# Relation scores of the edges by products of digit one-hots in the mean stage, and 32 gathered tiles in the second neighbour sum, in a four-layer graph network

## The chip, the cores and the metric

The kernel is written in Bass and runs as one program on one core of a Trainium2 chip. The metric is the device time of one execution in microseconds (us). TensorE is called PE here (its weight loads PEld), VectorE DVE, ScalarE ACT, GpSimd POOL, and the engine that only issues DMAs SP.

## What is computed

The graph has 12500 nodes, 200000 edges sorted by destination, 128 features and 200 edge types. Four layers follow each other, each with a residual sum and a layer norm. The parts that matter here:

```python
summed = segment_sum(feature[src], dst)            # layer 0: mean over incoming edges
agg = summed / max(deg, 1); h = relu(agg @ W.T) + feature
out = w[0] * h                                     # layer 1: complex, 32 neighbours a node, twice
for k in range(deg): out = out + w[1 + k] * h[nbrs[:, k]]
a = hs @ Ws.T + h[dst] @ Wd.T + emb_rel[etype] @ Wr.T      # layer 2: attention
e = leaky_relu((a @ attn_fc2_w.T)[:, 0], 0.01)     # softmax over the edges of a node, weighted sum
```

The third term of `a`, once multiplied by `attn_fc2_w`, is one number for each of the 200 relations. The kernel has these 200 numbers early (`rel_score`, on every partition) and needs for each edge the number of its type (`edge_score`).

## The kernel before

Nodes lie in 98 tiles of 128. Edges lie in 1660 steps (`STEPS`) of 128, each of which belongs to one tile; edge data is held as 128 partitions by 1664 columns, one column a step. All five engines run hand-written programs in order, joined by semaphores. In time the stages are these:

- **Preparation** (to about 370 us of the span): indices, degrees, weights.
- **Mean stage** (about 367 to 2520 us): for every step POOL gathers 128 rows of x (`sum_gpsimd`, L1014, a ring of 14 slots), ACT makes a one-hot of the destinations in two passes (L1026, L1028, 8 slots), PE multiplies (L1039) into one of four banks of PSUM (`N_SUM_BANKS`), and DVE adds the bank to the tile's sum (L1072). PE's product of step i waits until the sum of step i-4 is taken, and DVE's program adds step i-2 where PE's has step i. The **sort** of the neighbour lists shares DVE, PE and ACT: a stage is an ACT copy of 2048 columns to PSUM (L1175) and two DVE operations of 2048 columns (L1098, L1099) or four of 1024 (L1107, L1108), a turn is four PE transposes (L1146) and an ACT copy (L1179). `weave` lays the 10 items of a small side computation (`evo_vector`) and 333 items of the sort evenly over the 1660 steps, so that an item comes every 4.84 steps whatever it costs. The sort begins with 80 stages in a row.
- **finish0** (to about 2730 us): the dense part of layer 0 and the first layer norm.
- **First neighbour sum** (about 2730 to 4994 us): two laps over 52 dense tiles (`DENSE`), each 98 products of 384 columns (L1413); the matrices of counts are built in the first lap (DVE one-hots L1386 and L1391, PE L1399, ACT L1405), stored, and read back in the second. The other 46 tiles are gathered by POOL (L1449) and reduced by DVE (L1471). The ends of tiles (L1551 and on, PE L1688 to L1695) are spread over both laps.
- **Second neighbour sum** (about 4994 to 6396 us, `window2_*`): `SECOND = 28` tiles are gathered: 4 batches a tile, 8 gathers a batch (L1743), three batch slots, each batch reduced by DVE (L1756). The 70 others are dense: 52 with stored counts, then 18 whose counts are built beside their products (32 groups a tile, from `b == ROUND` on).
- **Attention** (about 6400 to 8750 us) and the convolution of layer 3 (to the end).

The relation scores are made on DVE by `rel_vector`: 200 pairs of passes over 1660 columns, one that picks the edges of relation r (L1712) and one that adds them to `edge_score` (L1714). 70 pairs (`EARLY_RELATIONS`) are woven into the second lap of the first sum, 130 into the second sum up to the point where its counts are built; `hot_vector(ROUND)` waits for the last of them, and so do the load of the late entries on SP and the attention.

## Time and profile before

| | us |
|---|---|
| median of 3 runs | 10004.24 |
| lowest and highest | 9991.14, 10006.8 |
| span of the profiled execution | 9988.2 |
| busy: PE, DVE, ACT, POOL | 7824.2, 7971.0, 5963.0, 6961.9 |
| first neighbour sum, second lap (about) | 3907 to 4994 |
| second neighbour sum (about) | 4994 to 6396 |

The profiled execution's time is known by its span alone, 9988.2 us, which is 16 us under the median of the runs and 3 us under the lowest. In the profile, a group of instructions shows its busy time, the mean duration of one in ns, and the idle time of its engine just before them with what ended it. PEclk is the granted TensorE clock as a share of 2.4 GHz. Rows that end in "xN" count instructions. A matmul on f32 operands shows as two records.

### The profile page before, as it was taken

Reading aid. Unit: us, or ns where it says so; the run is one execution under the profiler, and the core shown is the slowest. Engines: PE = TensorE matmul, PEld = TensorE weight load, DVE = VectorE, ACT = ScalarE, POOL = GpSimd, SP = SyncE. Lnnn points to the kernel's source line nnn. Section 1 sums busy time; section 2 is a strip of 40 time slices with the busy share of each in tenths; the row PEclk is TensorE's granted clock in tenths of the full one; section 3 lists DMA queues with packets and bytes.
Section 4 is the critical chain, followed back from the end, with each engine's and each line's share of the span. In section 5 each row is a group of like instructions: output and inputs, shape, how many; then the busy total and the mean of one; then the engine's idle time right before and its main releaser. Section 6 shows DMA issues by size and latency. Waiting matters only on the chain.

```text
span 9988.2 us, 178573 instructions
## 1 busy us (share of the span) xinstructions
PE 7824.2 (78%) x39865; PEld 6121.3 (61%) x39865; DVE 7971.0 (80%) x24833; ACT 5963.0 (60%) x18344; POOL 6961.9 (70%) x7476
## 2 busy tenths in 40 slices
PE   4444555555799999898889989888888888848887
PEld 4333444444477777777677777666666666636665
DVE  7787556555878887999967768788888888899999
ACT  6777777777877774111100006688888888846665
POOL 0466777777078887777678877566666666649995
PEclk6555555555899999999999999855565565557876
DMA  2222222222588888887766662322222222210000
GB/s 52 54 48 48 53 53 53 53 53 53 189 253 239 243 238 267 287 289 280 247 250 224 224 214 61 81 49 49 49 50 49 49 50 49 50 28 1 1 1 27
DMA packets 530133, 1151.52 MB, mean 115 GB/s; under 512 B 147134, under 2 KB 398210, under 8 KB 508750
## 3 DMA queue, kind: packets, MB, share of 16 engines
q0 software_dynamic: 241872, 477.23, 19.9%
q10 hardware_dynamic: 22752, 517.02, 13.2%
q1 hardware_dynamic: 264478, 145.85, 5.5%
q8 instruction: 363, 5.95, 0.2%
q14 instruction: 668, 5.47, 0.2%
HBM read 886.72 MB, written 259.31 MB: 115 GB/s over the span
## 4 chain that ended last, share of the span: by engine, by line
DVE 24%; POOL 23%; PE 22%; issue 14%; ACT 11%; DVEq 3%; DMA 2%; SPq 1%; ACTq 0%; POOLq 0%
POOL onehot L2185 9%; PE bank L1413 7%; POOL step_data L1743 7%; POOL step_data L1449 4%; PE bank_tile L2042 3%; POOL gather_ring L1449 3%; ACT onehot L1028 2%; DVE keys L1099 2%; DVE keys L1108 2%; ACT onehot L1026 2%; PE bank L1039 2%; DVE keys L1471 2%; DVE arena L1072 2%; PE bank_tile L2052 2%; DVE keys L2022 2%
## 5 line engine op out<-in xcount | busy, mean ns | idle before, releaser
L1014 POOL DMA_INDIRECT gather_ring<-mean_rows,step_data x1660 | 1596.1, 961 | 784.3 <-PE bank L1039 288.2
L1039 PE MATMUL bank<-gather_ring,onehot 128*128 128x130 f32 x3320 | 1042.1, 460 | 1053.0 <-DVE arena L1072 724.8
L1413 PE MATMUL bank<-arena 128*128 128x384 bf16 x8526 | 1628.5, 330 | 30.4 <-DMA arena<-split_out 26.9
L1413 PE MATMUL bank<-arena,keys 128*128 128x384 bf16 x8526 | 1623.5, 330 | 11.8 <-DMA arena<-split_im 11.8
L1039 PEld LDWEIGHTS bank<-gather_ring,onehot 128*128 128x128 f32 x3320 | 805.8, 306 | 1279.1 <-issue 851.6
L1413 PEld LDWEIGHTS bank<-arena 128*128 128x128 bf16 x8526 | 1178.9, 139 | 289.8 <-issue 47.5
L1413 PEld LDWEIGHTS bank<-arena,keys 128*128 128x128 bf16 x8526 | 1177.4, 138 | 270.5 <-issue 24.7
L1743 POOL DMA_INDIRECT step_data<-next_rows,window_idx x896 | 1045.9, 1167 | 351.1 <-issue 263.9
L1449 POOL DMA_INDIRECT step_data<-hidden,window_idx x888 | 1060.9, 1195 | 293.9 <-issue 265.9
L1966 POOL DMA_INDIRECT gather_ring<-attention_rows,step_data x834 | 786.8, 943 | 435.5 <-PE bank_tile L2042 228.6
L1966 POOL DMA_INDIRECT keys<-attention_rows,step_data x826 | 779.3, 943 | 388.0 <-PE bank_tile L2042 227.1
L1072 DVE TENSOR_TENSOR arena<-arena,bank 128x130 f32 x1660 | 482.4, 291 | 690.4 <-PE bank L1039 528.1
L2185 POOL TENSOR_SCALAR onehot<-iota_row,step_data 128x128 f32<-128x128 f32 x1660 | 960.0, 604 | 0.3 <-PE bank_tile L2223 0.2
L2213 ACT ACTIVATE gather_ring<-gather_ring,window_idx 128x128 f32<-128x128 f32 x1660 | 666.1, 401 | 295.7 <-DVE gather_ring L2196 268.9
L1449 POOL DMA_INDIRECT gather_ring<-hidden,window_idx x584 | 694.6, 1189 | 177.9 <-issue 174.3
L2196 DVE SCALAR_TENSOR_TENSOR gather_ring<-first_row,keys,l3b 128x128 f32<-128x128 f32 x1660 | 710.4, 428 | 0.2
L1028 ACT ACTIVATE onehot<-onehot,ones 128x128 f32<-128x128 f32 x1660 | 666.6, 402 | 53.8
L1026 ACT ACTIVATE onehot<-iota_row,step_data 128x128 f32<-128x128 f32 x1660 | 642.7, 387 | 93.6 <-PE bank L1039 67.5
L2084 ACT ACTIVATE step_small<-arena,step_small 128x1 f32 x1660 | 491.3, 296 | 315.3 <-DVE step_small L2012 289.4
L2052 PE MATMUL bank_tile<-ident,keys 128*128 128x128 f32 x1328 | 582.6, 439 | 120.6 <-DVE keys L2022 112.7
L1204 ACT ACTIVATE small<-small,eps 128x1 f32<-128x1 f32 x392 | 119.9, 306 | 893.8 <-DVE small L1200 882.1
L2004 DVE SCALAR_TENSOR_TENSOR arena<-arena,step_small,bank_tile 128x129 f32 x1328 | 465.5, 351 | 207.3 <-ACT step_small L2084 96.9
(350 smaller groups left out, 20302.8 us busy)
## 6 DMA issues: line engine op xcount, KB each, us to landing
keys<-count_rows ACTq DMA_DIRECT2D x50, 3136.0 KB
arena<-count_rows ACTq DMA_DIRECT2D x50, 3136.0 KB
count_rows<-arena ACTq DMA_DIRECT2D x26, 3136.0 KB
count_rows<-keys ACTq DMA_DIRECT2D x26, 3136.0 KB
gather_ring<-mean_rows,step_data POOLq DMA_INDIRECT x1660, 2.5
step_data<-next_rows,window_idx POOLq DMA_INDIRECT x896
step_data<-hidden,window_idx POOLq DMA_INDIRECT x888
gather_ring<-attention_rows,step_data POOLq DMA_INDIRECT x834
```

Of the source, the lines that this page charges most:

```text
L1014: e.indirect_dma_start(ring_at(rings.slot(name, i), SUM_COLS, SUMS - 1), None, rows, bass.IndirectOffsetOnAxis(src_idx[:, i:i + 1], 0), bo ...
L1026: e.activation(h, iota_row[:, :], ACT.Abs, bias=dst_local[:, j:j + 1], scale=-1.0).then_inc(hot_made)
L1028: e.activation(h, h, ACT.Relu, bias=ones[:, 0:1], scale=-1.0).then_inc(hot_made)
L1039: e.matmul(pass_bank[i % N_SUM_BANKS][:, 0:SUMS], onehot[:, i % STEP_SLOTS, :], ring_at(rings.slot(name, i), SUM_COLS, SUMS), start=True, ...
L1072: e.tensor_tensor(part, part, pass_bank[j % N_SUM_BANKS][:, 0:SUMS], ALU.add).then_inc(step_added)
L1413: m = e.matmul(pass_bank[n % 2][:, 0:SPLIT_COLS], counts[t % 2][:, :, h], split[:, h, :], start=(h == 0), stop=(h == NODE_TILES - 1))
L1449: e.indirect_dma_start(first_rows(i)[:, a, :], None, hidden1, bass.IndirectOffsetOnAxis(gather_idx[:, k * GATHERED + j:k * GATHERED + j + ...
L1743: e.indirect_dma_start(batch_rows[:, i % BATCH_SLOTS, r, :], None, next_rows, bass.IndirectOffsetOnAxis(gather_idx[:, at:at + 1], 0), boun ...
L1966: e.indirect_dma_start(attention_row(j), None, attention_rows, bass.IndirectOffsetOnAxis(src_idx[:, j:j + 1], 0), bounds_check=None).then_inc(
L2052: e.transpose(turned_part(j), logit[:, s, :], ident[:, :]).then_inc(a_logit_turned)
L2185: e.tensor_scalar(onehot[:, j % CONV_SLOTS, :], iota_row[:, :], dst_local[:, j:j + 1], None, ALU.is_equal).then_inc(hot_made)
L2196: e.scalar_tensor_tensor(lines[:, j % CONV_SLOTS, :], first_row[:, :], edge_coef[:, j:j + 1], l3b1[:, :], ALU.mult, ALU.add).then_inc(conv ...
```

## The change

`rel_vector` is replaced. A relation is split into a high digit (type modulo 8) and a low digit (type divided by 8, 0 to 24). The edge types are also written to DRAM in row form and read back four rows at a time. For each of the 128 rows, DVE makes a one-hot of the high digits (104 partitions by 128 columns, bf16) and one of the low digits (128 by 25 by 13, bf16); PE multiplies the first with a table split into three bf16 pieces (three products of 325 columns, summed in the fourth bank); DVE multiplies the result with the second and sums 25 values for each of 13 columns. This runs beside the mean, in `weave`, between `evo_vector` and the sort. The scores go to DRAM and are loaded again at the start of the second sum, as the late entries are. The mean has three banks instead of four. `weave` now gives every side item a cost, and the 1660 steps are shared in proportion: a stage 66 (6.9 steps), a turn 8 (0.83), a rescale 24, a row of relations 14 (1.46), an item of `evo_vector` 15 (1.56). `SECOND` is 32: 66 dense tiles, 14 of them with counts built, and 128 more gathers.

```diff
+N_SUM_BANKS = 3
...
-SECOND = 28
+SECOND = 32
...
-EARLY_RELATIONS = 70
+REL_HIGHS = 8
+REL_LOWS = RELATIONS // REL_HIGHS
+REL_PARTS = REL_HIGHS * STEP_GROUPS
+REL_COLS = REL_LOWS * STEP_GROUPS
+REL_ROWS = 4
+REL_LOADS = P // REL_ROWS
+REL_ROOM = 164
+REL_ROW_SLOTS = 2
+STAGE_COST, SHORT_COST, TURN_COST, RESCALE_COST, REL_COST = 66, 15, 8, 24, 14
...
+def weave(main, side, main_total, costs):
+    total, spent, at = sum(costs), 0, 0
+    for done, _ in enumerate(main, 1):
+        while at < len(costs) and spent * main_total < done * total:
+            next(side)
+            spent, at = spent + costs[at], at + 1
+    for _ in side:
+        pass
...
-SORT_STAGES = len(SORT) + 1 + DEG // 4 + GROUPS // 4
+SIDE_COSTS = [SHORT_COST] * 10 + [REL_COST] * (P + 2) + [
+    {"stage": STAGE_COST, "turn": TURN_COST, "rescale": RESCALE_COST}[row[0]] for row in SORT] + [
+    STAGE_COST] + [TURN_COST] * (DEG // 4 + GROUPS // 4)
...
-            own().tensor_copy(edge_rows_f[s][:, 2 * P:], edge_rows_sb[s][:, 2 * P:]).then_inc(n.sem, n.up())
+            own().tensor_copy(type_staged[:, g * P:(g + 1) * P], edge_rows_sb[s][:, 2 * P:]).then_inc(n.sem, n.up())
...
+    def rel_vector(e):
...
+        own().tensor_copy(type_int, type_staged).then_inc(n.sem, n.up())
+        own().tensor_scalar(type_int, type_int, REL_HIGHS - 1, None, ALU.bitwise_and).then_inc(n.sem, n.up())
+        own().tensor_copy(type_staged, type_int).then_inc(n.sem, n.up())
+        mark["types_staged"] = n.n
+        own().tensor_copy(type_int, edge_type[:, :]).then_inc(n.sem, n.up())
+        own().tensor_scalar(type_int, type_int, REL_HIGHS.bit_length() - 1, None,
+                            ALU.logical_shift_right).then_inc(n.sem, n.up())
+        own().tensor_copy(edge_type[:, :], type_int).then_inc(n.sem, n.up())
+        yield
+        own().tensor_copy(rel_iota, iota_row[:, 0:REL_LOWS].rearrange("p (w o) -> p w o", o=1).to_broadcast(
...
+        e.wait_ge(rel_landed, 32 * REL_HIGHS)
+        rest = rel_block[0:REL_PARTS, :]
...
+        for k in range(PIECES):
+            own().tensor_copy(rel_pieces[k][0:REL_PARTS, :], rest).then_inc(n.sem, n.up())
+            if k < PIECES - 1:
+                own().tensor_tensor(rest, rest, rel_pieces[k][0:REL_PARTS, :], ALU.subtract).then_inc(n.sem, n.up())
+        mark["rel_pieces"] = n.n
...
+        for r in range(P + 1):
+            if r < P:
+                c, at = divmod(r, REL_ROWS)
+                if at == 0:
+                    e.wait_ge(type_landed[c % REL_ROW_SLOTS], 16 * (c // REL_ROW_SLOTS + 1))
+                if r >= 2:
+                    e.wait_ge(rel_summed, r - 1)
+                    e.wait_ge(rel_scored, 2 * r - 3)
+                e.tensor_scalar(rel_hot[r % 2][0:REL_PARTS, :],
+                                rel_rows[c % REL_ROW_SLOTS][0:REL_PARTS, at * P:(at + 1) * P],
+                                rel_high[0:REL_PARTS, 0:1], None, ALU.is_equal).then_inc(rel_hots)
+                e.tensor_tensor(
+                    rel_low[r % 2],
+                    low_digits[:, r:r + 1, :].to_broadcast([P, REL_LOWS, STEP_GROUPS]),
+                    rel_iota, ALU.is_equal).then_inc(rel_hots)
+            if r:
+                i = r - 1
+                e.wait_ge(rel_summed, r)
+                e.wait_ge(rel_hots, 2 * r)
+                if i:
+                    e.wait_ge(rel_scored, 2 * i)
+                e.tensor_tensor(rel_product, rel_sums, rel_low[i % 2].rearrange("p w g -> p (w g)"),
+                                ALU.mult).then_inc(rel_scored)
+                e.wait_ge(rel_scored, 2 * i + 1)
+                e.tensor_reduce(scores[:, i, :], rel_product.rearrange("p (w g) -> p g w", w=REL_LOWS), AX.X,
+                                ALU.add).then_inc(rel_scored)
+            yield
+    def rel_tensor(e):
+        yield
+        yield
+        e.wait_ge(rel_digits.sem, mark["rel_pieces"])
+        for r in range(P):
+            e.wait_ge(rel_hots, 2 * r + 1)
+            if r:
+                e.wait_ge(rel_scored, 2 * r - 1)
+            for k in range(PIECES):
+                m = e.matmul(rel_sums, rel_hot[r % 2][0:REL_PARTS, :], rel_pieces[k][0:REL_PARTS, :],
+                             start=(k == 0), stop=(k == PIECES - 1))
+            m.then_inc(rel_summed)
+            yield
+    def rel_sync(e):
+        e.wait_ge(prep_copies, ACT_WEIGHTS)
+        with nc.allow_non_contiguous_dma(reason="one element a row, once"):
+            for h in range(REL_HIGHS):
+                e.dma_start(rel_table[h * STEP_GROUPS:(h + 1) * STEP_GROUPS, :],
+                            rel_score[0:STEP_GROUPS, :].rearrange("p (w h) -> p w h", h=REL_HIGHS)[:, :, h]).then_inc(
+                    rel_landed, 16)
+        e.wait_ge(rel_digits.sem, mark["types_staged"])
+        for h in range(REL_HIGHS):
+            e.dma_start(type_rows[h * STEP_GROUPS:(h + 1) * STEP_GROUPS, :, :].rearrange("g p e -> p g e"),
+                        type_staged.rearrange("p (g e) -> p g e", g=STEP_GROUPS)).then_inc(rel_landed, 16)
+        e.wait_ge(rel_landed, 32 * REL_HIGHS)
+        for c in range(REL_LOADS):
+            s = c % REL_ROW_SLOTS
+            if c >= REL_ROW_SLOTS:
+                e.wait_ge(rel_hots, 2 * (c - REL_ROW_SLOTS + 1) * REL_ROWS)
+            e.dma_start(rel_rows[s][0:REL_PARTS, :].rearrange("p (r e) -> p r e", r=REL_ROWS),
+                        type_rows[:, c * REL_ROWS:(c + 1) * REL_ROWS, :]).then_inc(type_landed[s], 16)
+        e.wait_ge(rel_scored, 2 * P)
+        e.dma_start(score_rows[:, :], made_score).then_inc(entries_saved, 16)
...
-        own().memset(edge_score, 0.0).then_inc(n.sem, n.up())
-        for r in range(RELATIONS):
-            own().tensor_scalar(picked, edge_type[:, 0:STEPS], float(r), rel_score[:, r:r + 1], ALU.is_equal,
-                                ALU.mult).then_inc(n.sem, n.up())
-            own().tensor_tensor(edge_score, edge_score, picked, ALU.add).then_inc(n.sem, n.up())
-            yield
...
                 if b == ROUND:
-                    e.wait_ge(rel_steps.sem, mark["rel_end"])
-                    e.wait_ge(entries_back, 16)
+                    e.wait_ge(entries_back, 32)
...
+        e.wait_ge(digit_steps, DIGITS * DENSE)
+        e.dma_start(entries_late, entry_rows[:, :]).then_inc(entries_back, 16)
+        e.wait_ge(built, ROUND)
+        e.dma_start(edge_score, score_rows[:, 0:STEPS]).then_inc(entries_back, 16)
...
-                if t == DENSE - 4:
-                    e.wait_ge(rel_steps.sem, mark["rel_end"])
-                    e.dma_start(entries_late, entry_rows[:, :]).then_inc(entries_back, 16)
...
-        weave(sum_vector(e, "mean", 0, regs), itertools.chain(evo_vector(e), sort_vector(e)), STEPS, EVO_STAGES + SORT_STAGES)
+        weave(sum_vector(e, "mean", 0, regs), itertools.chain(evo_vector(e), rel_vector(e), sort_vector(e)), STEPS, SIDE_COSTS)
...
-        relations = rel_vector(e)
-        weave(first_vector(e), itertools.islice(relations, EARLY_RELATIONS), 2 * ROUND + HOT_AHEAD, EARLY_RELATIONS,
-              ROUND + HOT_AHEAD + GROUPS)
-        weave(window2_vector(e), relations, ROUND - 2 * HOT_AHEAD, RELATIONS - EARLY_RELATIONS)
+        for _ in first_vector(e):
+            pass
...
+        weave(sum_tensor(e, "mean", 0), itertools.chain(range(EVO_STAGES), rel_tensor(e), sort_tensor(e)), STEPS, SIDE_COSTS)
...
+        weave(sum_scalar(e, 0), itertools.chain(evo_scalar(e), range(P + 2), sort_scalar(e)), STEPS, SIDE_COSTS)
```

## Rows read from the trace of the kernel before

**Rows 1.** The page: busy tenths of DVE and POOL in 40 slices of 250 us.
```profile
DVE  7787556555878887999967768788888888899999
POOL 0466777777078887777678877566666666649995
```
**Rows 2.** Windows (busy PE, PEld, DVE, ACT, POOL; PEclk; DMA share; GB/s), mean stage.
```profile
450.00:950.00 500.00, 204.24 (x711) 175.21 (x709) 427.40 (x627) 388.67 (x790) 342.79 (x362) 0.50 0.22 48
1000.00:2500.00 1500.00, 830.24 (x2842) 654.77 (x2842) 872.25 (x1484) 1108.26 (x2590) 1139.65 (x1183) 0.53 0.24 53
```
**Rows 3.** Groups of instructions, 340 to 2300 us, forms kept apart.
```profile
L1014 POOL DMA_INDIRECT gather_ring<-mean_rows,step_data x1489 | 1431.0, 961 | 732.1 <-PE bank L1039 259.0 <-issue 243.5 <-DMA mean_rows<-edge_values 229.7
...
L1072 DVE TENSOR_TENSOR arena<-arena,bank 128x130 f32 x1487 | 432.2, 291 | 626.3 <-PE bank L1039 479.9 <-DVE arena L1072 145.1 <-issue 0.9
```
**Rows 4.** Line L1014: ns min/median/max, first and last start.
```profile
L1014 POOL DMA_INDIRECT gather_ring<-mean_rows,step_data x1660: 938/944/4672, 366.7 to 2516.4; - x185
```
**Rows 5.** The timeline after a stage of the sort: start us, us, what.
```profile
904.19 0.28 DVE L1072 TENSOR_TENSOR arena<-arena,bank 128x130 f32 x1
...
904.62 2.74 PE L1039 MATMUL bank<-gather_ring,onehot 128*128 128x130 f32 x10 [3.83 <-DVE arena L1072]
904.68 0.29 DVE L1072 TENSOR_TENSOR arena<-arena,bank 128x130 f32 x1 [0.20 <-DVE arena L1072]
...
906.36 2.28 DVE L1098 TENSOR_TENSOR keys<-keys,bank_tile 128x2048 f32<-128x2048 f32 x1
```
**Rows 6.** The two passes of a relation, by line.
```profile
L1712 DVE TENSOR_SCALAR window_idx<-edge_type,rel_score x200: 1052/1078/1309, 3934.5 to 5939.8; 128x1660 f32<-128x1660 bf16 x100
L1714 DVE TENSOR_TENSOR keys<-keys,window_idx x200: 1886/1887/1891, 3935.8 to 5940.9; 128x1660 f32<-128x1660 f32 x100
```
**Rows 7.** POOL's gathers in 3960 to 4950, 5100 to 5900 and 6000 to 6300 us.
```profile
L1449 POOL DMA_INDIRECT step_data<-hidden,window_idx x420 | 458.5, 1092 | 129.6 <-issue 125.8 <-DVE keys L1471 3.8
...
L1743 POOL DMA_INDIRECT step_data<-next_rows,window_idx x507 | 648.3, 1279 | 154.5 <-issue 154.2 <-DVE gather_ring L1756 0.3
...
L1743 POOL DMA_INDIRECT step_data<-next_rows,window_idx x218 | 211.8, 971 | 89.7 <-issue 59.4 <-DVE gather_ring L1756 30.4
```
**Rows 8.** The second lap: its window, and PE's longest wait there (us, times, longest).
```profile
3907.00:4994.00 1087.00, 956.51 (x5552) 775.65 (x5552) 997.71 (x1717) 125.40 (x380) 813.22 (x742) 0.95 0.78 278
...
PE bank_tile L1688 <- DVE turned_few L1567: 105.6, 45, 6.5
```
**Rows 9.** The second sum: lines L1743 and L1413; then windows of L1413 and of L1399.
```profile
L1743 POOL DMA_INDIRECT step_data<-next_rows,window_idx x896: 938/945/3022, 4998.6 to 6354.5; - x180
...
L1413 PE MATMUL bank<-arena,keys x8526: 325/326/528, 2774.2 to 6391.9; 128*128 128x384 bf16 x199
...
6000.00:6100.00 100.00, 93.61 (x435) 60.33 (x435) 1.00 0.25 64
...
6000.00:6100.00 100.00, 46.83 (x142) 16.00 (x143) 1.00 0.25 64
```
**Rows 10.** DVE groups of the whole span that are nearest to the new operations.
```profile
L2031 DVE TENSOR_SCALAR keys<-iota_half,step_data 128x128 bf16<-128x128 bf16 x1660 | 452.4, 273 | 6.3 <-issue 5.7 <-PE bank L2059 0.5
L1386 DVE TENSOR_TENSOR onehot<-arena,iota_quad 128x512 bf16<-128x512 bf16 x560 | 236.5, 422 | 254.5 <-PE bank_tile L1399 249.8 <-issue 0.2
...
L1756 DVE TENSOR_REDUCE gather_ring<-step_data 128x128 f32<-128x1024 f32 x112 | 219.1, 1956 | 115.9 <-DMA step_data<-next_rows,window_idx 115.9
...
L601 DVE TENSOR_TENSOR keys<-arena,iota_half 125x784 bf16<-125x784 bf16 x120 | 116.2, 968 | 0.0
```
**Rows 11.** SP's issue of 12544 single elements; a window inside the load of x.
```profile
L986 SPq DMA_DIRECT2D mean_rows<-edge_values x1: 387/387/387, 348.7 to 348.7; - x1
...
385.00:390.00 5.00, 3.07 (x9) 1.98 (x9) 1.88 (x10) 4.81 (x13) 3.78 (x5) 0.50 1.05 290
```
**Rows 12.** The timeline at 5045 us: a relation's pass and a gather.
```profile
5045.57 1.89 DVE L1714 TENSOR_TENSOR keys<-keys,window_idx 128x1660 f32<-128x1660 f32 x1
5045.97 2.31 POOL L1743 DMA_INDIRECT step_data<-next_rows,window_idx  x1 [0.30 <-issue]
```

More of the change, by code:

```diff
@@ L120, in landed @@
         return self.sems[s], 16 * (self.base[name][s] + sum(self.sizes[name][s:i + 1:self.slots[name]]))
-def weave(main, side, main_total, side_total, after=0):
-    done_main = done_side = 0
-    for _ in main:
-        done_main += 1
-        while side is not None and done_side * (main_total - after) < (done_main - after) * side_total:
-            if next(side, StopIteration) is StopIteration:
-                side = None
-            done_side += 1
-    if side is not None:
-        for _ in side:
-            pass
+def weave(main, side, main_total, costs):
[6 more added lines that the diff above has]
+        pass
 def ending(now, hop):
@@ L472, in program @@
     batch_added = sem("gathered_batch_added")
-    rel_steps = Tally(sem("relation_score_steps"))
+    rel_digits = Tally(sem("relation_digit_steps"))
+    rel_landed = sem("relation_tables_landed")
+    type_landed = [sem(f"type_rows_landed{i}") for i in range(REL_ROW_SLOTS)]
+    rel_hots = sem("relation_onehots")
+    rel_summed = sem("relation_products")
+    rel_scored = sem("relation_score_steps")
     hist_high = sem("source_high_onehots")
@@ L835, in prep_tensor_program @@
             e.wait_ge(prep_vector.sem, mark["edges_read", g])
-            for k in range(3):
+            for k in range(2):
                 e.transpose(tile_bank[2 + s][:, k * P:(k + 1) * P], edge_rows_f[s][:, k * P:(k + 1) * P],
                             ident[:, :]).then_inc(made)
+            e.transpose(tile_bank[2 + s][:, 2 * P:2 * P + P // 2].bitcast(BF16), type_staged[:, g * P:(g + 1) * P],
+                        ident_half[:, :]).then_inc(made)
             if g >= 1:
@@ L2316, in tensor @@
         e.wait_ge(prep_vector.sem, mark["setup"])
-        weave(sum_tensor(e, "mean", 0), itertools.chain(range(EVO_STAGES), sort_tensor(e)), STEPS, EVO_STAGES + SORT_STAGES)
+        weave(sum_tensor(e, "mean", 0), itertools.chain(range(EVO_STAGES), rel_tensor(e), sort_tensor(e)), STEPS, SIDE_COSTS)
         finish0_tensor(e)
@@ L2342, in sync @@
         x_program(e)
+        rel_sync(e)
         sort_sync(e)
```

65 lines of the change are left out of this document (51 added, 14 removed).

## The prediction

> **What bounds the kernel now.** I read the page's slices first [rows 1]: DVE stands at 9 in slices 17 to 20, where 70 of the relation pairs lie, and at 6 or 7 in 21 to 24 with the other 130; POOL stands at 7 or 8 through most of the mean stage and of both sums. Then the windows.
>
> In the mean stage POOL sets the pace. A gather takes 0.944 us with about 0.30 between two: 1.25 us a step at best. From 366.7 to 2516.4 us its 1660 gathers take 2150 us, 1.296 each, so 75 us lie above that floor [rows 4]. The window from 450 to 950, where the sort's 80 first stages lie, has 362 gathers in 500 us, 1.38 each, with DVE busy for 427; the one from 1000 to 2500 has 1183, 1.268 each, with DVE at 58% [rows 2]. So DVE bounds the stretch where stages come densely, POOL the rest. A stage blocks DVE for 4.6 us, and 0.29 us adds follow it, 0.20 apart [rows 5]; POOL's ring of 14 hides about 17 us of delay.
>
> In the second lap of the first sum, DVE is busy for 998 of 1087 us and POOL makes 742 gathers, 1.42 us each with hardly a wait, since each takes 1.092 instead of 0.944 [rows 7, 8]. PE waits 105.6 us for ends that come late from DVE [rows 8]. In the second sum the gathers take 1.279 us while relations run and 0.971 after [rows 7]; DVE waits for their landing (115.9 us in all) [rows 10]. There POOL, slowed by DVE, holds the others. After 6000 us PE is full: 435 products and 142 counts in 100 us, 0.173 us each [rows 9].
>
> **Part 1, the 200 pairs go.** DVE loses 200 x (1.078 + 1.887) = 593 us [rows 6], of which 70 pairs, 207 us, lie in the lap and 130, 386 us, in the second sum. DVE time by itself is worth nothing; two things follow from it.
>
> In the lap, POOL's gathers fall from 1.09 to about 0.96 us, 1.26 with the gap: 742 x (1.42 - 1.26) = 119 us less for POOL. PE gets back up to the 105.6 us it waits, and has then no more idle time: it needs about 1087 - 106 = 981 us. Next late is PE itself, at full work. I take 95 us off the lap; bounds 40 (the waits of PE are only moved, as DVE still has some 790 us of work there) and 110.
>
> **Part 2, 32 gathered tiles.** POOL now has 1024 gathers in the second sum. They start at 4998.6 and end at 6354.5, and the stage ends some 40 us later [rows 9]. Without relations one costs 0.96 + 0.30: 1024 x 1.262 = 1292 us, and 11 us that POOL waits at the start for its slots come again. POOL ends at 4998.6 + 1303 = 6302, the stage at about 6340: 56 us earlier. PE has 66 x 98 = 6468 products and 14 x 32 = 448 counts, 6916 x 0.173 = 1196 us, ended well before that; so the four tiles more lie on POOL's path, and it becomes the one bound of the stage. Bounds: 20 (gathers at 1.30) and 75 us (1.25).
>
> **Part 3, the relation rows enter the mean stage.** The new code lies at steps 16 to 206 of 1660: costs 150 + 130 x 14 of a total of 15936, that is 9.6 a step.
>
> Before the first row stand six passes over 1664 columns on DVE, priced by [rows 6] at 1.1 to 1.9 us, some 9 us; then a wait for 16 DMAs. Eight are small. The other eight write the digits to DRAM in 13312 pieces of 256 bytes, and SP issues them after the load of x (6.4 MB at 290 GB/s, to about 400) [rows 11]. The nearest price below is 12544 single elements in 366.7 - 348.7 = 18 us [rows 4, 11]; above, x itself, 12500 pieces of 512 bytes in 22 us, and half as much again is 33. The ten early items now come every 1.56 steps, so DVE reaches the digits at about 407, has them at 412 and the first rows of digits back at about 440. POOL's ring covers 17 us of that stop. The 32 reads of four rows are prefetched by 4 to 8 rows, over 10 us: nothing. If that cover goes, a landing of 2 to 3 us stands on each fourth row, about 80 us in all.
>
> One row on DVE: one-hot of 128 columns 0.27; one-hot of 325 columns 0.37 (bounds 422 x 325/512 = 0.27 and 968 x 325/784 = 0.40); product of 325 columns 0.49 (slope between 0.291 at 130 and 1.887 at 1660 columns); sum 0.62 (325/1024 of 1.956; bounds 0.49 at the product's price and 0.75) [rows 3, 6, 10]. That is 1.75, and 0.20 between the dependent two [rows 5]: 1.95. With 1.46 adds of 0.29 it is 2.4 to 2.5 us, against 1.82 that POOL needs for 1.46 steps. So DVE becomes the bound there. PE can add to it. Its three products of 325 columns at half clock [rows 2] take 3 x 0.173 x 2 x 325/386 = 0.88 us, and with three banks its mean product of step i waits for the add of step i-3, which DVE makes only one step ahead. In a row that spans two steps (46% of them) the chain is: sum 0.82, add 0.29, mean product 0.7, three products 0.9, product 0.49, latencies: 3.3 us. A row with one step takes 2.24. The mean is 2.73. I take 2.6, between this and DVE's own 2.47; bounds 1.9 and 3.2.
>
> 128 x 2.6 = 333: the rows end at 773. What is left is 1455 steps, of which 14 are already gathered: 1441 x 1.265 = 1823 (as 1.268 now; dense stages have 6.9 steps, 8.6 us, for 4.6 of stage and some 3.4 of adds, so three banks just suffice). Turns get only 0.83 steps, 1.04 us, less than their transposes and a mean product take on PE; the ring absorbs eight in a row. The stage ends at 2600 against 2520: **80 us later**. Bounds: 243 for the rows and 1.25 after, 32 us earlier; 410 and 1.30, 207 us later.
>
> A rule bears on these rows. One gather that began beside an addition of two SBUF operands took 2.31 us instead of 0.94 [rows 12]. The Trainium skill (GPSIMD Engine Reference, Key points) says that GpSimd shares its SBUF interfaces with VectorE and contends with instructions in a two-port mode or with two SBUF inputs; by that, row and rule agree, and it speaks against the change: the one-hot of 325 columns has two SBUF inputs. By rows 12 the two one-hots would hold POOL for up to 0.64 us a row, 1.82 + 0.64 = 2.46: hidden behind DVE's 2.6, but it takes most of the gain away should rows be cheap.
>
> Everything else I put at nothing: preparation swaps a cast for a cast; two loads of 0.2 and 0.8 MB at the start of the second sum lie beside 30 us of waiting for the split rows; ACT has no new work in the rows, and SP waits in them with nothing urgent behind it (the sort's entries come at its end).
>
> **Sum.** +80 - 95 - 56 = -71. The profiled execution's 9988 becomes 9917. The median of the runs lies 16 us above its span, so I forecast 10004 - 71 = **9933 us**. A measurement of this kernel can tell about 0.2%, 20 us, from no change.
>
> **Rivals.**
> - *Rows at POOL's pace* (0.17). If sum and one-hot stand at their low bounds and PE keeps ahead, the mean stage ends 32 us early: -32 - 95 - 56 = -183, 9821. For it: PE at half clock is busy for only 41% of 450 to 950 [rows 2]. Against: 1.95 + 0.42 is over 1.82 by any middle price.
> - *Rows held by the exchange of DVE and PE* (0.19), the other side. Each row passes DVE, PE, DVE, and the three banks tie the mean to the same chain. At 3.7 us a row the stage ends 80 + 128 x 1.1 = 220 us later: +69, 10073. It decides from 3.3 us a row: 80 + 90 is then over 151 + 19. For it: PE already waits behind DVE's adds for 3.83 us at a time [rows 5]. Against: one-step rows don't have the long chain.
> - *The sums give back little* (0.16). The lap yields only 40, as PE is just as busy, and the second sum 30, as 128 gathers fill the room: +80 - 70 = +10, 10014. For it: PE is busy for 957 of the lap's 1087 us [rows 8]. Against: its 105.6 us of waiting end in DVE's work.
> - That relations still stand in the sums can't be: their loop is gone.
>
> **How the numbers follow.** My forecast has 0.48. Faster by over 0.2%: 0.48 + 0.17 and 0.01 of the third, 0.66. Within: 0.13 of the third. Slower: 0.19 and 0.02 of the third, 0.21. The forecast's own range, from its bounds, is 9870 to 9980; with the rivals up to two in ten left out it reaches from 9830 to 10050.
>
> **What would show it.** Right: the last mean gather near 2597, rows of relations from about 440 to 773 with some 2.6 us between two products of DVE, POOL under 1.30 us a gather up to there lost and 1.265 after; gathers of 0.95 to 0.97 us in both sums; the lap at about 990 us; POOL without waits in the second sum and PE with some. Wrong: rows under 2 or over 3.3 us, DVE stopped for over 60 us before the first row, the mean stage above 1.30 after the rows (turns or three banks), or a second sum that ends no sooner than now.

## The result and the profile after

The changed kernel takes **10085.93 us**, median of 4 runs (10082.44 to 10087.5), against 10000.3 us of the kernel before in the same session (9991.14 to 10006.8): a ratio of **1.0085**, 95% interval 1.0071 to 1.01. It is slower. The forecast was 9933, the range ended at 10050, and slower had 0.21. The profiled execution has a span of 10080.7 us, 92.5 more than the 9988.2 of before. In six of the twelve sessions on record the kernel before itself took 10.9 to 11.0 ms instead of 10.0, so each run below is set against the kernel before of its own session, and only runs within a session, or from sessions in which it took 10.0 ms, are compared.

First the slices of the page, which answer to [rows 1]: DVE is no longer at 9 in slices 17 to 20 and only at 5 to 3 in 21 to 24, but in the mean stage POOL has come down too, from 7 to 6 in slices 5 to 10.

```profile
DVE  7776666666687888688853336788888888899999
...
POOL 0256666666617888777767777666666666649995
```

Then the gathers of the mean stage (min/median/max ns, first and last start), which answer to [rows 4].

```profile
L1051 POOL DMA_INDIRECT gather_ring<-mean_rows,step_data x1660: 938/944/4668, 374.3 to 2801.6; - x185
```

The last one starts at 2801.6 us instead of 2516.4: 285 us later, where 80 were forecast. Windows of the changed kernel (busy PE, PEld, DVE, ACT, POOL; PEclk; DMA share; GB/s): the rows of relations, the sort behind them, the second lap of the first sum, the second sum.

```profile
450.00:750.00 300.00, 224.44 (x714) 131.54 (x714) 234.53 (x657) 143.71 (x355) 167.62 (x178) 0.50 0.23 53
800.00:2500.00 1700.00, 701.72 (x2782) 626.82 (x2782) 1085.26 (x1691) 1186.00 (x2648) 1152.69 (x1199) 0.55 0.22 47
4194.00:5170.00 976.00, 923.55 (x5552) 771.81 (x5552) 798.49 (x1574) 125.82 (x380) 714.85 (x744) 0.99 0.86 310
5170.00:6500.00 1330.00, 1200.18 (x7210) 978.06 (x7210) 640.21 (x1953) 258.22 (x645) 976.51 (x1028) 0.96 0.58 197
```

From 800 to 2500 us there are 1199 gathers, **1.42 us each**; before it was 1.268 [rows 2]. No engine is full: ACT is at 70%, POOL 68%, DVE 64%, PE 41%. The lap lasts 976 us instead of 1087 [rows 8], with PE busy for 95% of it. The second sum goes from 5177.1 to the last product at 6488.3, 1311 us, where it was 4998.6 to 6391.9, 1393 [rows 9]. The balance: +285 in the mean stage, -111 in the lap, -82 in the second sum, together +92; the first lap and all that follows the sums stayed.

The waits of the changed kernel from 800 to 2750 us (us in all, times, longest) say who stands still in that mean stage.

```profile
PE bank L1076 <- DVE arena L1109: 1132.9, 200, 13.1
ACT onehot L1063 <- PE bank L1076: 512.5, 184, 6.0
POOL gather_ring L1051 <- PE bank L1076: 356.1, 484, 6.0
...
DVE keys L1239 <- ACT bank_tile L1317: 182.4, 100, 7.6
DVE keys L1248 <- ACT bank_tile L1317: 175.2, 81, 6.8
```

It is a ring: PE waits for DVE, ACT and POOL wait for PE, and DVE waits for ACT. The two rows at the end are the new ones. They are the sort's own operations waiting for ACT's copy of the stage, 357.6 us together; the same two waits of the kernel before (L1098 and L1107 on L1175) come to 32.9 us in that window. The timeline of one cycle of the changed kernel (start us, us, engine, line; in brackets the idle time before it) shows how the ring closes.

```profile
1449.98 0.28 DVE L1109 TENSOR_TENSOR arena<-arena,bank 128x130 f32 x1
1450.41 3.72 PE L1076 MATMUL bank<-gather_ring,onehot 128*128 128x130 f32 x14 [5.60 <-DVE arena L1109]
...
1451.22 0.40 ACT L1063 ACTIVATE onehot<-iota_row,step_data 128x128 f32<-128x128 f32 x1 [2.74 <-PE bank L1076]
...
1451.96 0.39 ACT L1063 ACTIVATE onehot<-iota_row,step_data 128x128 f32<-128x128 f32 x1
...
1452.69 0.39 ACT L1063 ACTIVATE onehot<-iota_row,step_data 128x128 f32<-128x128 f32 x1
1452.92 0.29 DVE L1109 TENSOR_TENSOR arena<-arena,bank 128x130 f32 x1 [0.20 <-DVE arena L1109]
...
1453.41 1.86 ACT L1317 ACTIVATE bank_tile<-keys 128x2048 f32<-128x2048 f32 x1
...
1455.31 2.29 DVE L1239 TENSOR_TENSOR keys<-keys,bank_tile 128x2048 f32<-128x2048 f32 x1 [2.10 <-ACT bank_tile L1317]
...
1457.51 2.28 DVE L1240 TENSOR_TENSOR keys<-keys,bank_tile 128x2048 f32<-128x2048 f32 x1
...
1459.71 0.28 DVE L1109 TENSOR_TENSOR arena<-arena,bank 128x130 f32 x1
```

At 1449.98 DVE leaves its block (the two operations of a stage, in which it takes no sums) and takes seven sums, 0.49 us apart, to 1453.21. PE had stood for 5.60 us, since all three banks were full; ACT had stood for 2.74, since its eight one-hots were made and none used. The stage's input has been ready since the block ended, but its copy starts only at 1453.41: in ACT's program three one-hots stand ahead of it, and each needs a product of PE. Then DVE waits 2.10 us for the copy. A cycle is 3.23 (sums) + 2.10 + 4.40 (block) = 9.73 us for seven steps, 1.39 a step.

### The profile page after: what moved, and what is told of

Same layout as the page of the kernel before. It is cut to its first block, busy times and chain, and to the rows that moved or that the text cites. A ratio compares the mean times of both kernels' runs of the same rounds, so it can differ in the third digit from the quotient of the medians.

```text
span 10080.7 us, 178575 instructions
## 1 busy us (share of the span) xinstructions
PE 7676.8 (76%) x39729; PEld 6052.8 (60%) x39729; DVE 7613.9 (76%) x24805; ACT 5912.3 (59%) x18216; POOL 6791.2 (67%) x7604
## 4 chain that ended last, share of the span: by engine, by line
POOL 29%; PE 19%; DVE 18%; issue 14%; ACT 13%; DMA 3%; DVEq 2%; SPq 1%; ACTq 0%; POOLq 0%
POOL onehot L2307 10%; POOL step_data L1865 8%; POOL step_data L1591 7%; POOL gather_ring L1591 4%; PE bank L1555 4%; ACT bank_tile L1317 3%; PE bank_tile L2164 3%; PE bank L1076 3%; ACT onehot L1065 2%; DVE keys L1240 2%; ACT onehot L1063 2%; DVE keys L1249 2%; PE bank_tile L2174 2%; DMA step_data<-hidden,window_idx 2%; DVE keys L2144 2%
## 5 line engine op out<-in xcount | busy, mean ns | idle before, releaser
L1076 PE MATMUL bank<-gather_ring,onehot 128*128 128x130 f32 x3320 | 948.6, 451 | 1320.5 <-DVE arena L1109 1214.7
L1555 PE MATMUL bank<-arena 128*128 128x384 bf16 x8330 | 1579.2, 329 | 28.6 <-DMA arena<-split_out 26.5
L1555 PE MATMUL bank<-arena,keys 128*128 128x384 bf16 x8330 | 1567.7, 328 | 10.0 <-DMA arena<-split_im 10.0
L1555 PEld LDWEIGHTS bank<-arena 128*128 128x128 bf16 x8330 | 1149.6, 138 | 275.7 <-issue 43.5
L1555 PEld LDWEIGHTS bank<-arena,keys 128*128 128x128 bf16 x8330 | 1147.6, 138 | 250.1 <-issue 20.7
L1865 POOL DMA_INDIRECT step_data<-next_rows,window_idx x1024 | 972.7, 950 | 351.4 <-issue 309.3
L1591 POOL DMA_INDIRECT step_data<-hidden,window_idx x888 | 999.3, 1125 | 293.6 <-issue 265.2
L1591 POOL DMA_INDIRECT gather_ring<-hidden,window_idx x584 | 655.9, 1123 | 177.9 <-issue 176.4
```

The lines of the kernel that those rows point to most:

```text
L1076: e.matmul(pass_bank[i % N_SUM_BANKS][:, 0:SUMS], onehot[:, i % STEP_SLOTS, :], ring_at(rings.slot(name, i), SUM_COLS, SUMS), start=True, ...
L1555: m = e.matmul(pass_bank[n % 2][:, 0:SPLIT_COLS], counts[t % 2][:, :, h], split[:, h, :], start=(h == 0), stop=(h == NODE_TILES - 1))
L1591: e.indirect_dma_start(first_rows(i)[:, a, :], None, hidden1, bass.IndirectOffsetOnAxis(gather_idx[:, k * GATHERED + j:k * GATHERED + j + ...
L1865: e.indirect_dma_start(batch_rows[:, i % BATCH_SLOTS, r, :], None, next_rows, bass.IndirectOffsetOnAxis(gather_idx[:, at:at + 1], 0), boun ...
```

## The experiments

**Theory A.** What counts is how far ACT can get while DVE is in its block. PE stops after as many products as there are banks, ACT after eight one-hots more (the eight slots), and since it makes one-hots `HOT_LEAD` = 5 steps ahead, the copy that stands s steps behind the block in the program is reached only if s is at most banks + 6 - lead (8 slots less the 2 steps by which DVE's sums lag): 5 in the kernel before, 4 after. Stages come every 4.84 steps before and every 6.9 after. So both edits, the third bank given away and the weave by costs, push the copy behind DVE's sums. **Theory B:** the weave alone does it. **Theory C** (used later): the missing bank itself does it, whatever ACT's order.

### Three banks alone, in the kernel before

```diff
-    N_SUM_BANKS = len(pass_bank)
+    N_SUM_BANKS = 3
```

> The kernel before with three banks for the mean instead of four, and nothing else. Theory A (the sort's copy on ScalarE stands in program order behind one-hots that wait for TensorE's products, and these for banks that VectorE has yet to add; so banks and the number of steps between two stages decide together): in runs of stages a five-step cycle gets one one-hot later, 0.7 us, the mean stage ends 60 to 130 us later than 2520, the time rises by as much. Theory B (the turns' small share of steps and the weights of the weave alone slow the changed kernel, banks are irrelevant): the mean stage ends within 20 us of 2520.

11220.37 us against 11033.23, +187. Again, on another chip:

> The kernel before with three banks for the mean, taken again. Theory A: in runs of stages the copy waits for one one-hot more in a cycle with five steps, and the block and its adds were the bound there already: the mean stage ends 60 to 130 us after 2520. Theory B (three banks suffice at any spacing): within 20 us.

11084.8 against 10905.17, +180. Both are more than the 60 to 130 us that theory A had given. A third time:

> The kernel before with three banks of the mean instead of four (N_SUM_BANKS), nothing else. Theory A (the copy of a sort stage stands on ScalarE behind one-hots that wait for a bank): the copy can stand at most 4 steps ahead instead of 5, and stages come every 4.84 steps, so a part of it falls behind each dense stage: the last mean gather from 2516 to 2560-2700 and the time from 10004 to 10050-10180. The theory of the prediction (three banks just suffice): 2516-2530, 10004-10020.

**10174.12 us** (3 runs) against 9996.34: 1.0177, 1.0157 to 1.0197. The gathers of this kernel:

```profile
L1014 POOL DMA_INDIRECT gather_ring<-mean_rows,step_data x1660: 938/944/4584, 368.0 to 2692.4; - x185
```

its waits from 400 to 2500 us:

```profile
ACT onehot L1026 <- PE bank L1039: 439.3, 171, 5.9
...
DVE keys L1107 <- ACT bank_tile L1175: 119.0, 84, 3.3
DVE keys L1098 <- ACT bank_tile L1175: 114.4, 87, 2.8
```

and the same waits of the kernel before with its four banks:

```profile
ACT onehot L1026 <- PE bank L1039: 63.0, 86, 3.4
DVE keys L1107 <- ACT bank_tile L1175: 20.2, 17, 3.3
DVE keys L1098 <- ACT bank_tile L1175: 14.8, 19, 2.9
```

One bank less costs 178 us, and the last gather comes 176 us later. DVE's wait for the copy grows by 198 us, ACT's for PE by 376. Nothing else was touched: even at the old spacing of the stages three banks don't suffice.

### The weave by costs alone, in the kernel before

```diff
-        weave(sum_vector(e, "mean", 0, regs), itertools.chain(evo_vector(e), sort_vector(e)), STEPS, EVO_STAGES + SORT_STAGES)
+        weave_costs(sum_vector(e, "mean", 0, regs), itertools.chain(evo_vector(e), sort_vector(e)), STEPS, SIDE_COSTS)
```

(the same for PE and ACT; costs as in the change, without the rows)

> The kernel before, its mean woven by the costs of the change (stage 66, turn 8, rescale 24, early item 15), four banks, relation passes where they were. A stage then has 7.8 steps, a turn 0.94. Theory A: the copy waits for some three one-hots after VectorE's block, but a cycle has 9.7 us of gathers to hide it in: the mean stage ends between 2470 and 2550 us. Theory B: turns that get 0.94 steps slow the stretches with turns to over 1.40 us a step, the mean stage ends after 2650.

11082.46 us against 11033.23, +49. Again:

> The kernel before woven by the costs of the change, four banks, taken again. Theory A: 7.8 steps lie between stages, the copy comes three one-hots late, about as long as 9.7 us of gathers can hide: the mean stage ends between 2470 and 2550. Theory B (the turns with 0.94 steps each are too tight): it ends after 2650.

10926.3 against 10905.17, +21. Theory B, that the weave alone makes the loss, is not supported by these single runs. The last gathers came at 2832.2 and 2812.0, past the 2470 to 2550 of theory A and where the rival of too tight turns had put them (after 2650); but no trace shows where the kernel before has its last gather when it takes 10.9 ms or more, so this decides nothing. DVE does wait for the copy in both (128.4 and 130.1 us from 800 to 2750, where the kernel before at 9988.2 waits 32.9), so the weave isn't free of A's effect with four banks either; a run against 10.0 ms would be needed for its size.

### The changed kernel with an even sort, and with a lead of 2

```diff
-STAGE_COST, SHORT_COST, TURN_COST, RESCALE_COST, REL_COST = 66, 15, 8, 24, 14
+STAGE_COST, SHORT_COST, TURN_COST, RESCALE_COST, REL_COST = 42, 15, 42, 42, 14
```

> The changed kernel with the same cost, 42, for each item of the sort (4.4 steps each), three banks. Theory A: the copy is hardly late, but VectorE's block and 4.4 adds take 6.7 to 7 us against 5.5 us of gathers, 1.55 us a step in 190 stages, and 1.25 in the rest: the mean stage ends at 2780 to 2830, no gain. Theory B (turns too tight is what slows it): it ends 100 us or more earlier than 2805.

11583.89 us against 11033.23, last gather at 3034.9: inconclusive, as the changed kernel itself was not run against 11033.23.

```diff
-    HOT_LEAD, ADD_LAG = 5, 2
+    HOT_LEAD, ADD_LAG = 2, 2
```

This kernel, the changed one with a lead of 2, was run in five sessions.

> The changed kernel with the one-hots made two steps ahead in program order instead of five. Theory A: ScalarE comes to the copy three steps earlier, so the copy starts as soon as VectorE's block ends and the 2 us that VectorE waits for it are gone; a stage's cycle falls from 9.73 us to what 6.9 gathers take, 8.6 us; the mean stage ends at 2570 to 2620 instead of 2805, the time is about 9860 to 9910. Theory B: no change, within 20 us.

> The changed kernel with the one-hots two steps ahead instead of five, three banks, taken again while the kernel before runs at its usual 10000 us. Theory A (the copy stands behind one-hots that wait for banks): the copy starts when VectorE's block ends, a stage's cycle falls from 9.73 to about 8.6 us, the mean stage ends at 2570 to 2620. Rival C (the shorter lead starves TensorE of one-hots where turns and relation rows lie): it ends above 2700.

> The changed kernel, three banks, with the one-hots two steps ahead instead of five. Theory A (the copy stands behind one-hots that wait for banks): the copy starts when VectorE's block ends, a stage's cycle falls from 9.73 to about 8.6 us, the mean stage ends at 2570 to 2620. Rival C (the shorter lead starves TensorE of one-hots): it ends above 2700.

> The changed kernel (three banks) with the destination one-hots made 2 instead of 5 steps ahead (HOT_LEAD), nothing else. Theory A (the copy of a sort stage stands on ScalarE behind one-hots that wait for a bank): with three banks and a lead of 2 the copy can stand 7 steps ahead, as with four banks and a lead of 3, so it starts right behind the block; DVE's wait for the copy, 357.6 us in all from 800 to 2750 us in the changed kernel, falls under 120; the last mean gather moves from 2802 to 2640-2720 and the time from 10086 to 9925-10005. Theory C (the bank itself is what is missing: PE stands still in the block after three products, not ScalarE's order): no gain, 2780-2820 and 10060-10100. Theory D (a lead of 2 starves PE of one-hots): over 2820.

> Again the changed kernel (three banks) with a one-hot lead of 2 instead of 5. Theory A (the copy stands behind one-hots that wait for a bank, so a shorter lead cures three banks as well as four): last mean gather 2640-2720 instead of 2802, time 9925-10005. Theory C (the missing bank itself holds PE in the block, whatever ScalarE's order): 2780-2820, 10060-10100. Theory D (a lead of 2 starves PE of one-hots): over 2820.

One run each in the first three: 11487.65 against 11033.23, 11346.06 against 10905.17, 11345.68 against 10898.65. The last two, of three runs each: 11464.7 against 11022.18 (1.0408, 1.0388 to 1.0429) and 11338.63 against 10898.14 (1.0412, 1.0391 to 1.0433). It is slower than the kernel before in all five; as the changed kernel wasn't run in them, the totals decide nothing between A and C, and whether a lead of 2 leaves PE short of one-hots (theory D) stays open. A stretch of the fourth run's timeline shows the mechanism of A all the same:

```profile
1456.54 0.28 DVE L1109 TENSOR_TENSOR arena<-arena,bank 128x130 f32 x1
1456.65 1.88 ACT L1317 ACTIVATE bank_tile<-keys 128x2048 f32<-128x2048 f32 x1 [1.33 <-DVE keys L1240]
...
1460.10 2.28 DVE L1239 TENSOR_TENSOR keys<-keys,bank_tile 128x2048 f32<-128x2048 f32 x1
...
1464.49 0.28 DVE L1109 TENSOR_TENSOR arena<-arena,bank 128x130 f32 x1
```

Now ACT waits for DVE, not DVE for ACT: the copy starts 0.11 us after the block, and a cycle of seven steps lasts 7.95 us instead of 9.73, with three banks.

### A fourth bank in the changed kernel

The fourth bank holds the rows' products only until the rows end; from step 240 on the mean can have it.

```diff
+    FOUR_FROM = 240
+    def sum_bank(i):
+        return pass_bank[i % (N_SUM_BANKS if i < FOUR_FROM else 4)]
...
-                if i >= N_SUM_BANKS:
-                    e.wait_ge(step_added, lap_ * STEPS + i - N_SUM_BANKS + 1)
+                if i == FOUR_FROM + 3:
+                    e.wait_ge(rel_scored, 2 * P)
+                banks = N_SUM_BANKS if i < FOUR_FROM + 3 else 4
+                if i >= banks:
+                    e.wait_ge(step_added, lap_ * STEPS + i - banks + 1)
```

> The changed kernel with a fourth bank for the mean from step 240 on, when the relation rows have left it. Theory A (ScalarE's copy stands behind one-hots that wait for banks): one more product can be made in VectorE's block, so the copy starts one one-hot earlier, 0.7 us of 9.7 a stage, over 190 stages some 140 us: the mean stage ends near 2650 to 2690 instead of 2805, the time is 9930 to 9980. Theory B (the turns' small share of steps slows it): within 20 us of the changed kernel.

**9965.72 us** (4 runs) against 10008.17: 0.9957, 0.9938 to 0.9977. The last gather comes at 2669.3, 132 us earlier than in the changed kernel. DVE's waits for the copy are 234.5 us from 800 to 2600 us (239.8 to 2750, against 357.6):

```profile
DVE keys L1255 <- ACT bank_tile L1324: 120.9, 81, 6.6
DVE keys L1246 <- ACT bank_tile L1324: 113.6, 98, 7.2
```

This restores the limit of 5 steps but not the spacing of 6.9, and half the wait for the copy is left in a cycle at the same place: 1.08 us of 9.12, where it was 2.10 of 9.73. That fits A, but C as well.

### Four banks and a lead of 3

```diff
-    HOT_LEAD, ADD_LAG = 5, 2
+    HOT_LEAD, ADD_LAG = 3, 2
```

This stands on top of the fourth bank of the run before. It ran three times. The first two:

> The changed kernel with the fourth bank from step 240 on and the one-hots three steps ahead. Theory A: by one bank and two steps of lead the copy is no more behind a waiting one-hot; a stage costs what its 6.9 gathers take; the mean stage ends at 2560 to 2600, the time is 9860 to 9900. Rival C (the shorter lead starves TensorE): no better than with the fourth bank alone, 9966.

> The changed kernel with the fourth bank from step 240 on and the one-hots three steps ahead, taken again. Theory A: the copy of a stage is no more behind a waiting one-hot; a stage costs what its 6.9 gathers take, 8.6 us; the mean stage ends at 2560 to 2600, the time is 9860 to 9900. Rival C (the shorter lead starves TensorE of one-hots): no better than with the fourth bank alone, 9966.

11334.23 against 10905.17 and 11316.83 against 10898.65, 4.0% and 3.9% slower than the kernel before; without the changed kernel beside them they decide nothing between the theories. The third:

> The changed kernel with a fourth bank from step 240 on (as in the run before) and destination one-hots made 3 instead of 5 steps ahead of the gather. Theory A (the copy of a sort stage stands on ScalarE behind one-hots that wait for a bank): with a lead of 3 and four banks the copy can stand up to 7 steps ahead, so it starts as soon as the last DVE operation of the block before it ends; the 1.08 us that DVE waits for the copy in each stage falls to under 0.3, a cycle of 7 steps from 9.12 to about 8.8 us (DVE's gap gone, then POOL's 7 x 1.25), the last mean gather moves from 2669 to 2610-2650 and the time to 9900-9950. Theory B (the weave by costs holds the stages, whatever the lead): 2669 and 9966 stay. Theory C (the shorter lead starves PE of one-hots): later than 2700, over 9990.

**9860.95 us** (3 runs) against 9997.11: 0.9864, 0.9845 to 0.9883, faster than theory A said. The last gather comes at 2581.4. From 800 to 2750 us DVE's waits for the copy are 52.2 us, and POOL makes 1344 gathers in the 1700 us from 800 to 2500, 1.265 each: it is the bound again.

### Three banks and a lead of 3: A against C

The changed kernel with the one line above, and nothing else.

> The changed kernel (three banks) with a one-hot lead of 3 instead of 5, nothing else. A fourth bank gave 132 us of the mean stage with a lead of 5, and the shorter lead then another 88. Theory A (what counts is how far the stage's copy can stand ahead on ScalarE, banks plus slots less lead): three banks and a lead of 3 let it stand 6 ahead, one more than four banks and a lead of 5, so the last mean gather comes at 2600-2669 instead of 2802 and the time is 9880-9966. Theory C (the missing bank itself holds PE in the block, whatever ScalarE's order): at most a third of the 220 us, 2730-2810 and 10020-10095.

**9863.49 us** (3 runs, 9859.24 to 9865.84) against 9995.54: 0.987, 0.9851 to 0.9889. Its gathers:

```profile
L1051 POOL DMA_INDIRECT gather_ring<-mean_rows,step_data x1660: 938/944/4603, 370.5 to 2581.8; - x185
```

and its waits from 800 to 2750 us:

```profile
PE bank L1076 <- DVE arena L1109: 710.4, 199, 10.8
ACT onehot L1063 <- PE bank L1076: 256.3, 197, 4.5
...
DVE keys L1248 <- ACT bank_tile L1317: 54.6, 52, 6.8
```

With L1239's 44.1 us DVE waits for the copy for 98.7 us instead of 357.6. The timeline shows one one-hot ahead of the copy where there were three:

```profile
1460.73 0.40 ACT L1063 ACTIVATE onehot<-iota_row,step_data 128x128 f32<-128x128 f32 x1 [1.28 <-PE bank L1076]
...
1461.48 1.86 ACT L1317 ACTIVATE bank_tile<-keys 128x2048 f32<-128x2048 f32 x1
...
1463.37 2.29 DVE L1239 TENSOR_TENSOR keys<-keys,bank_tile 128x2048 f32<-128x2048 f32 x1 [0.23 <-ACT bank_tile L1317]
```

C falls: without a fourth bank the mean stage is 220 us shorter, as short as with one (2581.8 and 2581.4), and even a little shorter than A had said (2600 to 2669). What the missing bank does, it does through ACT's order. At either spacing of the stages, the larger the limit, the earlier the last gather, until POOL is the bound:

| kernel | banks, lead | limit | stages every | last gather | time |
|---|---|---|---|---|---|
| before | 4, 5 | 5 | 4.84 | 2516.4 | 10000 |
| before, three banks | 3, 5 | 4 | 4.84 | 2692.4 | 10174 |
| changed | 3, 5 | 4 | 6.9 | 2801.6 | 10086 |
| changed, fourth bank | 4, 5 | 5 | 6.9 | 2669.3 | 9966 |
| changed, lead of 3 | 3, 3 | 6 | 6.9 | 2581.8 | 9863 |
| changed, both | 4, 3 | 7 | 6.9 | 2581.4 | 9861 |

### A lead of 3 in the kernel before

```diff
-    HOT_LEAD, ADD_LAG = 5, 2
+    HOT_LEAD, ADD_LAG = 3, 2
```

> The kernel before (four banks, relations in the sums, weave by count) with the destination one-hots made 3 instead of 5 steps ahead, nothing else. If the shorter lead helps only because the weave by costs packs up to 7 steps between two stages, it gives nothing here, where stages come every 4.84 steps and the copy can already stand 5 ahead: 2505-2525 for the last mean gather, 9990-10010. If the one-hots that wait for PE's banks hold ScalarE here too, the mean stage nears POOL's own pace of 1.25 us: 2445-2490, 9930-9980. If a lead of 3 starves PE where DVE's blocks come densely: over 2540 and 10020.

9991.7 us (9 runs) against 9993.21 (11 runs): 0.9997, 0.9986 to 1.0007. Last gather at 2516.7. DVE's waits for the copy from 800 to 2750 us are 26.8 us here, against 32.9 in the kernel before: with a limit of 5 and stages every 4.84 steps there is hardly a wait to remove, so the gain of the shorter lead belongs to the changed kernel. It follows that the spacing of 6.9 has a price with four banks too: the 88 us from 2669.3 to 2581.4. Freed of the waits, the change is worth -132 us (9863.49 - 9995.54).

### 28 gathered tiles instead of 32

```diff
-SECOND = 32
+SECOND = 28
```

(with a lead of 3)

> The changed kernel with a one-hot lead of 3 and 28 gathered tiles in the second sum instead of 32: the change without its second size. If POOL bounds the second sum with 32 tiles (1024 gathers of 0.95 and 0.30 us from 4959 to 6253, PE busy for 1197 of 1310 us), then with 28 its 896 gathers end after 1130 us, and PE with 520 more products and counts, some 87 us, needs 1284 of work and becomes the bound: the last dense product comes 1285 to 1330 us after the start instead of 1313, and the time is 9835-9880, no more than 20 us from 9863.5. If the four tiles more were worth what the prediction's second part says of them (the whole of its 56 us), it is 9900-9920.

11210.01 us against 10896.02, which can't be set beside the 9863.49: POOL waits for DVE here for 555.2 us in the second sum, which with 32 tiles, at 9863.49, it did for 11.0. How the 82 us of the second sum divide between the relations that left and the four tiles stays open.

## Why the prediction was wrong

**What failed: the pace after the rows.** Part 3 took "1441 x 1.265 (as 1.268 now; dense stages have 6.9 steps, 8.6 us, for 4.6 of stage and some 3.4 of adds, so three banks just suffice)". Block and sums were right (4.40 and 3.23 us), but they don't follow each other: 2.10 us of waiting for ACT's copy lie between them. 9.73 us for seven steps is 1.39 a step. Over all that follows the rows, the gathers took 2058 us (743.2 to 2801.6), 1.42 each, where 1823 had been foretold: this term was 235 us too small. The rows had come 30 us early, so the last gather missed the 2597 foretold by 205. The term's upper bound of 1.30 was the mean of the old stage, not a bound of the new one. I had named three banks as what could make the stage slow and never asked through whom: the sum counted the bank's effect on PE and DVE, and not on the third engine, whose program has the copy behind one-hots that need PE. The kernel before gave a sign of it: ACT's one-hots waited for PE for 63 us with a longest wait of 3.4. The lead of 3 shows that this was the step: it alone brings the pace to 1344 gathers in 1700 us, 1.265, and the last gather to 2581.8, against the 2597 foretold.

**Part 3, the rows: right.** DVE's wait for the digits' way through DRAM is 12.8 us (28 had been left for it, from 412 to 440), and the first product of DVE starts at 431.6. The operations of a row, from 431 to 744 us, forms kept apart:

```profile
L1179 DVE TENSOR_REDUCE window_idx<-window_idx 128x13 f32<-128x325 f32 x128 | 91.7, 716 | 4.4
...
L1176 DVE TENSOR_TENSOR window_idx<-bank,wide_few 128x325 f32<-128x325 f32 x128 | 62.8, 491 | 48.8 <-PE bank L1192 48.8
...
L1166 DVE TENSOR_TENSOR wide_few<-edge_type,narrow_few 128x325 bf16<-128x325 bf16 x127 | 42.8, 337 | 0.0
L1163 DVE TENSOR_SCALAR wide_few<-turned_few,narrow_few 104x128 bf16<-104x128 bf16 x126 | 34.1, 271 | 0.2 <-issue 0.2
```

Product 0.49 as foretold, the sum 0.72 instead of 0.62, the large one-hot 0.34 instead of 0.37; a row takes (743.2 - 431.6) / 127 = 2.45 us, against 2.6, and PE holds DVE up for 48.8 us in all. Both rivals of the rows fall: POOL's pace (1.9) and the exchange of DVE and PE (3.7).

**Part 1, the lap: right in kind, and close by luck.** 976 us against the 981 worked out from PE's waits, -111 against -95 (its bound was 110). But PE didn't get all its waits back. Its wait for the ends of tiles over the whole lap, before (3907 to 4994 us) and after (4194 to 5170; us, times, longest):

```profile
PE bank_tile L1688 <- DVE turned_few L1567: 111.0, 49, 6.5
...
PE bank_tile L1830 <- DVE turned_few L1709: 38.3, 27, 5.8
```

PE's idle time fell from 130 to 52 us, by 78. The other 33 us are PE's own work: the same 5552 records take 923.55 us instead of 956.51, at a granted clock of 0.99 instead of 0.95 [rows 8], and the prediction had no term for that. POOL's gathers fell to 714.85 / 744 = 0.961 us. (Its 742 gathers in 1087 us were 1.46 each before, not the 1.42 of the prediction, which its sum doesn't use.) The rival "the sums give back little" falls.

**Part 2, the second sum: right in kind, small by a third.** -82 against -56. The 1024 gathers take 1291 us from first to last start against 1303, 0.950 each, and POOL waits 10 us for DVE in all; the last product comes 20 us behind the last gather, not 40. The group of the second sum's gathers:

```profile
L1865 POOL DMA_INDIRECT step_data<-next_rows,window_idx x1024 | 972.7, 950 | 351.4 <-issue 309.3
```

**The numbers.** With the pace as it was assumed, the sum would have come to what the kernel with a lead of 3 shows: +65 in the mean stage and -189 behind it, 9864.1 against 9988.2 of span, where +80 and -151 were foretold. So even with that pace the time would have been 70 us under the forecast of 9933, mostly by the second sum. The chance of 0.21 for slower stood on the rows' exchange (0.19) and on little gain in the sums (0.02); a rival for "the sort's stages get slower with three banks" was missing, though the change takes a bank from a stage in which PE already waited 724.8 us for DVE (400 to 2500 us).

## What to carry to other kernels

When a change takes a buffer from a ring, or spaces out the items woven into it, don't ask only whether the two engines at that buffer still keep up: walk through the program of every engine that stands behind them in order, and count how far each can get while the bound engine is in its long block. Work that the bound engine will need next (here the copy of the sort's stage) must not stand behind work that needs what that block holds back; making the filler less far ahead was worth 220 us here for one digit in the source, and nothing in the kernel before. And the mean pace of a stage is no upper bound for a stage whose order changed: build the cycle from its own operations, the waits between them included.

## What the runs showed of the hardware that I had not expected

- **Which passes of DVE slow a gather.** The 0.64 us a row that I allowed for the one-hots weren't needed: from 431 to 744 us 185 gathers ran beside 127 large ones and took 945 ns on average. But this doesn't show that such a one-hot leaves a gather alone. Only three of the 185 began inside one, and they took 0.94, 1.11 and 0.94 us; the others began at another time. In the sort the case is clear. From 800 to 2500 us in the changed kernel 539 gathers began inside a pass of two operands whose second lies in PSUM (L1239, L1240, L1248, L1249), and all took 0.94 or 0.95 us; the 10 that began inside the pass over 4096 f32 columns of SBUF (L1234), with one tensor operand, took 2.62 to 2.96. So the contention that [rows 12] show, and of which the Trainium skill (GPSIMD Engine Reference, Key points) speaks, is seen here with long f32 passes over SBUF, of one operand too, and not with passes of up to 2.3 us that take their second operand from PSUM. First a gather inside a pass with PSUM, in the changed kernel, then one inside a pass over SBUF, in the kernel with four banks and a lead of 3:

```profile
1457.51 2.28 DVE L1240 TENSOR_TENSOR keys<-keys,bank_tile 128x2048 f32<-128x2048 f32 x1
1457.69 0.94 POOL L1051 DMA_INDIRECT gather_ring<-mean_rows,step_data  x1 [0.30 <-issue]
...
1450.91 2.42 DVE L1241 TENSOR_SCALAR keys<-keys,signs 128x4096 f32<-128x4096 f32 x1 [3.70 <-ACT keys L1328]
...
1451.52 2.62 POOL L1055 DMA_INDIRECT gather_ring<-mean_rows,step_data  x1 [0.30 <-issue]
```

- **Engines that stop together.** In the fourth run with a lead of 2 (11459.25 us) ACT, DVE and POOL stand still for 2.5 to 2.6 us and resume within 0.24 us of each other, with a release that the profile can't name ("remote"):

```profile
1450.85 0.40 ACT L1063 ACTIVATE onehot<-iota_row,step_data 128x128 f32<-128x128 f32 x1 [2.52 <-remote]
1450.95 0.29 DVE L1109 TENSOR_TENSOR arena<-arena,bank 128x130 f32 x1 [2.59 <-remote]
1451.09 0.95 POOL L1051 DMA_INDIRECT gather_ring<-mean_rows,step_data  x1 [2.60 <-remote]
```

From 800 to 2750 us POOL alone has 78 such waits there, 140.1 us; the traces of the kernel before at 9988.2 us, of the changed one and of the one with three banks and a lead of 3 at 9864.1 have none. What stops the engines wasn't found out, nor why the shorter leads come out slower than the kernel before in such runs.
